# Roots by power on GpSimd, products on zeros, 64-row row sums and sums over consecutive words in an attention and expert kernel

## The reference

```
# a: retention, per sequence, 8 heads
h = layernorm(x)
q, k, v, g = h @ wq, h @ wk / 4, h @ wv, h @ wg;  q, k rotated
qk = (q k^T) * decay mask;  qk = qk / max(|rowsum(qk)|, 1)
out = qk v;  out = out * rsqrt(mean(out^2 per head) + 1e-5)
x = x + (silu(g) * out) @ wo
# b: hidden = layernorm(x); attention ACROSS the 8 sequences at each token position, causal, 16 heads, 4 kv heads
h1 = hidden + proj(attention(layernorm(hidden)))
# c, m: top 2 of 8 experts, with a capacity of 640 tokens an expert
ln2 = layernorm(h1);  gates = softmax over the top 2 of ln2 @ router
x = x + h1 + sum_e gate_e * gelu(ln2 @ w1_e) @ w2_e
```

## Time and profile before

| | |
|---|---|
| median of 3 runs | 242.56 us (239.90 to 242.67) |
| the profiled execution | 242.57 us, its span 240.8 us |
| busy: PE, PE weight loads | 216.7 us (90%), 183.6 us |
| busy: DVE, ACT, POOL | 180.1 us (75%), 146.1 us (61%), 94.8 us (39%) |
| ACT table loads | 36, of 1283 ns |
| chain that ended last | PE 54%, DVE 16%, issue 14%, POOL 9%, ACT 4% |

### The profile page before, as it was taken

How to read it: one execution, slowest core, us unless ns; L and a number is a source line. 1 busy time by engine, 2 the same in 40 slices (tenths; PEclk the granted TensorE clock), 3 DMA queues, 4 the chain that set the end, 5 groups by cost and what they waited for, 6 DMA issues and landing times.

```text
span 240.8 us, 4945 instructions
## 1 busy us (share of the span) xinstructions
PE 216.7 (90%) x1744; PEld 183.6 (76%) x1744; DVE 180.1 (75%) x543; ACT 146.1 (61%) x268; POOL 94.8 (39%) x121
## 2 busy tenths in 40 slices
PE   0677868899999999989999999999999989989995
PEld 0456545688887878877888889998798869879994
DVE  1466788695989789899996998697749864895533
ACT  2162763778868756946973876586746465827431
POOL 0021345334558642528623850582465136521000
PEclk9977999999999999999999999999999999999999
DMA  6992000000000000000000000000000000000000
GB/s 178 292 319 57 4 0 0 4 0 3 0 3 3 0 25 0 3 1 3 1 0 25 0 0 4 22 3 0 22 3 1 23 0 4 22 3 0 23 3 22
DMA packets 8073, 6.46 MB, mean 27 GB/s; under 512 B 752, under 2 KB 7152, under 8 KB 8048
## 3 DMA queue, kind: packets, MB, share of 16 engines
q1 hardware_dynamic: 8048, 6.14, 8.8%
HBM read 5.09 MB, written 1.05 MB: 25 GB/s over the span
## 4 chain that ended last, share of the span: by engine, by line
PE 54%; DVE 16%; issue 14%; POOL 9%; ACT 4%; DMA 1%; DVEq 0%; POOLq 0%; ACTq 0%
PE bank L773 16%; PE bank L784 13%; POOL prod L293 5%; PE bank L672 3%; DVE ao L930 3%; PE bank L621 3%; PE bank L699 3%; PE bank L638 2%; DVE res L1036 2%; PE bank L684 2%; ACT L445 2%; POOL qk L369 2%; PE bank L629 1%; PE bank L691 1%; DVE sm L866 1%
## 5 line engine op out<-in xcount | busy, mean ns | idle before, releaser
L773 PE MATMUL bank<-x2T,w 128*128 128x256 f32 x256 | 64.4, 386 | 1.6 <-DVE res L1036 1.6
L784 PE MATMUL bank<-w,hT 128*128 128x128 f32 x512 | 64.7, 277 | 0.0
L784 PEld LDWEIGHTS bank<-w,hT 128*128 128x128 f32 x512 | 61.7, 192 | 3.0 <-issue 1.1
L583 ACT ACTIVATE hT<-bank 128x512 f32<-128x512 f32 x64 | 37.5, 598 | 23.6 <-PE bank L773 23.5
L773 PEld LDWEIGHTS bank<-x2T,w 128*128 128x128 f32 x256 | 45.3, 190 | 8.1 <-DVE res L1036 3.1
L1036 DVE SCALAR_TENSOR_TENSOR res<-bank,gate,res 128x128 f32<-128x128 f32 x128 | 38.4, 341 | 16.7 <-PE bank L784 15.4
L445 ACT ACT_TABLE_LOAD x36 | 46.2, 1283 | 4.4 <-DVE mv L812 3.7
L293 POOL TENSOR_TENSOR prod<-qkv 128x128 f32<-128x128 f32 (+7 forms) x16 | 22.3, 1413 | 36.6 <-ACT qkv L455 36.6
L866 DVE TENSOR_TENSOR sm<-bank,con 128x512 f32<-128x512 f32 x32 | 19.9, 683 | 5.1 <-PE bank L672 5.0
L301 POOL TENSOR_TENSOR prodv<-attn_exp,qkv 128x128 f32<-128x128 f32 (+7 forms) x16 | 18.7, 1188 | 9.2 <-ACT attn_exp L551 9.2
L376 POOL TENSOR_TENSOR qkc<-qk,kcum 128x256 f32<-128x256 f32 x8 | 5.8, 730 | 31.0 <-DVE kcum L852 31.0
(11 more groups left out here) (109 smaller groups left out, 378.8 us busy)
## 6 DMA issues: line engine op xcount, KB each, us to landing
x<-in_x SPq DMA_DIRECT2D x8, 128.0 KB, 4.3
w<-in_w SPq DMA_DIRECT2D x1, 1024.0 KB, 5.8
out<-res SPq DMA_DIRECT2D x8, 128.0 KB, 1.8
con<-in_consts SPq DMA_DIRECT2D x1, 512.0 KB, 4.2
con<-in_consts SPq DMA_DIRECT2D x1, 256.5 KB, 4.3
con<-in_consts SPq DMA_DIRECT2D x1, 256.0 KB, 4.4
rcon<-in_rconsts SPq DMA_DIRECT2D x1, 132.0 KB, 2.9
wqk<-in_wqk SPq DMA_DIRECT2D x1, 128.0 KB, 2.2
```

Source lines behind the costliest of these rows:

```text
L583: eng.activation(hT[:, n % NM], m_banks[n % NM][:].rearrange("p (t n) -> p t n", t=NF), ACT.Gelu_apprx_tanh).then_inc(sem("gelu"), 1)
L773: last = mm(m_banks[n % NM][:, t * SLEN:(t + 1) * SLEN], w1[:, e, t * P:(t + 1) * P], x2T[:, i], start=True, stop=True)
L784: last = mm(m_banks[n % NM][:, c * D:(c + 1) * D], hT[:, n % NM, t, c * P:(c + 1) * P], w2[:, e, t], start=(t == 0), stop=(t == NF - 1))
```

## The change

- `a_rstd`, `b_rstd`, `c_rstd` leave ACT. GpSimd adds eps (`tensor_scalar`) and raises to -0.5 (`tensor_tensor` with `pow` against a broadcast constant). Three constants fewer for ACT's bias, one more for the exponent.
- A new stage `p_warm` on PE, eight times in the order: a product of zeros into the first expert bank. DVE clears `warm` at the start.
- `a_rowsums` multiplies only the 64 feature rows that belong to each half of the heads, into two banks (`front` joins f0 and f1), and so waits for `silu`; `a_scores` no longer does.
- For sequences 0 and 1 DVE does `a_qkc`, `a_weight`, `b_core` (straight from x1 with mean and root), `b_prod`, `b_prodv`.
- Scores, exponentials and V products are laid out with the sequence index `t` innermost, so `b_max`, `b_sum`, `b_ao` read consecutive words; `b_scores` writes with a stride, and `value_product` reads V with a stride of one sequence (192 words).
- The whole `ORDER` is written anew.

```diff
@@ ORDER (both listings are some 78 lines; the start of each)
-a_stats:0 a_aggr:0 a_rstd:0 a_xh:0 a_T:0 a_xT:0 a_qk:0 a_vmm:0 a_rotate:0 a_v:0 a_rotated:0 a_stats:1 a_kT:0
-a_aggr:1 a_knat:0 a_kcum:0 a_rstd:1 a_state_mm:0 a_stats:2 a_qkc:0 a_g:0 a_stats:3 a_state:0 a_aggr:2 a_xh:2
-a_rowsums:0 a_tanh:0 a_qo:0 a_silu:0 a_s2:0 a_xh:1 a_aggr:3 a_scores:0 a_mask:0 a_rstd:2 a_T:1 a_xT:1 a_qk:1
+p_warm:0 p_warm:1 p_warm:2 a_stats:0 p_warm:3 a_aggr:0 a_rstd:0 a_xh:0 a_T:0 a_xT:0 a_qk:0 a_vmm:0 a_rotate:0
+a_v:0 a_g:0 a_rotated:0 p_warm:4 a_tanh:0 a_kcum:0 a_kT:0 a_knat:0 a_qo:0 a_silu:0 a_state_mm:0 p_warm:5 a_qkc:0
+a_state:0 a_stats:1 a_rowsums:0 a_aggr:1 a_rstd:1 a_s2:0 a_scores:0 a_xh:1 a_stats:2 a_mask:0 p_warm:6 a_T:1
...
@@ GpSimd
+            def root(o, i_, n):
+                return eng.tensor_tensor(o, i_, minus_half[:].to_broadcast([P, n]), ALU.pow)
+
+            def b_rstd(i):
+                eng.wait_ge(sem("b_aggr"), NC * (i + 1))
+                eng.tensor_scalar(bln[:, i, :, 0], bmv[:, i, :, 1], EPS, None, ALU.add).then_inc(sem("b_var"), 1)
+                eng.tensor_scalar(bln[:, i, :, 1], bmv[:, i, :, 1], 1.0 + EPS, EPS * EPS,
+                                  ALU.mult, ALU.add).then_inc(sem("b_var"), 1)
+                eng.wait_ge(sem("b_var"), 2 * (i + 1))
+                root(br[:, i].rearrange("p c k -> p (c k)"), bln[:, i].rearrange("p c k -> p (c k)"),
+                     2 * NC).then_inc(sem("b_rstd"), 1)
...
@@ value_product
-                prodv[:, c, 0:n * D].rearrange("p (a d) -> p a d", d=HD),
-                attn_exp[:, c * n * NH:(c + 1) * n * NH].unsqueeze(2).to_broadcast([P, n * NH, HD]),
-                qkv[:, c, 0:n, D + KVD:QKV].unsqueeze(2).to_broadcast([P, n, QPK, KVD]), ALU.mult)
+                prodv[:, c, 0:n * D].rearrange("p (h d t) -> p h d t", d=HD, t=n),
+                attn_exp[:, c * n * NH:(c + 1) * n * NH].rearrange("p (h t) -> p h t", t=n)
+                .unsqueeze(2).to_broadcast([P, NH, HD, n]),
+                qkv[:, c, 0:n, D + KVD:QKV].rearrange("p t f -> p f t")
+                .unsqueeze(1).to_broadcast([P, QPK, KVD, n]), ALU.mult)
...
@@ TensorE
+            def p_warm(i):
+                if i == 0:
+                    eng.wait_ge(sem("warm"), 1)
+                mm(m_banks[0][:, 0:SLEN], warm[:, 0:P], warm[:], start=True, stop=True)
...
             def a_rowsums(i):
                 eng.wait_ge(sem("qkc"), i + 1)
                 eng.wait_ge(sem("state"), i + 1)
+                eng.wait_ge(sem("silu"), i + 1)
                 for u in range(2):
-                    last = mm(f1[:, u * SLEN:(u + 1) * SLEN], same_head[:, u * P:(u + 1) * P], qkc[:],
+                    rows = slice(u * D // 2, (u + 1) * D // 2)
+                    last = mm(front[:, u, 0:SLEN], same_head[rows, u * P:(u + 1) * P], qkc[rows, :],
                               start=True, stop=True)
...
@@ VectorE
+            def b_core(i):
+                if i < VECTOR_FIRST:
+                    eng.wait_ge(sem("b_rstd"), i + 1)
+                    if i >= 1:
+                        eng.wait_ge(sem("b_T"), i)
+                    for c in range(NC):
+                        last = ts_(core[:, c], x1[:, i, c], bmv[:, i, c, 0:1], br[:, i, c, 1:2], ALU.subtract, ALU.mult)
+                    last.then_inc(sem("core"), 1)
...
@@ b_scores, b_ao
-                    eng.tensor_reduce(sc[:, c * n * NH:(c + 1) * n * NH],
-                                      prod[:, c, 0:n * D].rearrange("p (a d) -> p a d", d=HD),
+                    eng.tensor_reduce(sc[:, c * n * NH:(c + 1) * n * NH].rearrange("p (h t) -> p t h", t=n),
+                                      prod[:, c, 0:n * D].rearrange("p (t h d) -> p t h d", t=n, d=HD),
                                       X, ALU.add).then_inc(sem("sc"), 1)
...
-                    eng.tensor_reduce(ao[:, c], prodv[:, c, 0:n * D].rearrange("p (t f) -> p f t", t=n),
+                    eng.tensor_reduce(ao[:, c], prodv[:, c, 0:n * D].rearrange("p (f t) -> p f t", t=n),
                                       X, ALU.add).then_inc(sem("ao"), 1)
```

More of the change, by code:

```diff
@@ L49 @@
[L49 to L53, removed]
@@ L276, in build @@
         res = sb("res", [P, NSEQ, NC, D])
-        ps = [ctx.enter_context(nc.psum_tensor(f"bank{i}", [P, 512], F32)) for i in range(8)]
+        front = ctx.enter_context(nc.psum_tensor("bankf", [P, 2, 512], F32))
+        ps = [front[:, 0], front[:, 1]] + [ctx.enter_context(nc.psum_tensor(f"bank{i}", [P, 512], F32))
+                                           for i in range(2, 8)]
         f0, f1, k0, k1 = score_banks = ps[:4]
@@ L455, in copy @@
                 eng.copy(o, i_).then_inc(sem(name), 1)
-            def a_rstd(i):
-                group = next(g for g in RSTD_GROUPS if g[0] == i)
-                eng.wait_ge(sem("a_aggr"), NC * (group[-1] + 1))
-                if i == 0:
-                    eng.wait_ge(sem("eps"), 2)
-                exp_ln()
-                js = slice(group[0], group[-1] + 1)
-                eng.activation(lnv[:, js], mv[:, js, :, 1], ACT.Ln, bias=eps[:, 0:1]).then_inc(sem("a_lnv"), 1)
-                eng.wait_ge(sem("a_lnv"), RSTD_GROUPS.index(group) + 1)
-                eng.activation(rstd[:, js], lnv[:, js], ACT.Exp, scale=-0.5).then_inc(sem("a_rstd"), len(group))
             def a_xT(i):
@@ L660, in a_scores @@
                 eng.wait_ge(sem("qo"), i + 1)
-                eng.wait_ge(sem("silu"), i + 1)
                 eng.wait_ge(sem("s2"), i + 1)
@@ L853, in a_kcum, with a_qkc, a_weight, b_prod @@
                                        ALU.add).then_inc(sem("kcum"), 1)
+            def a_qkc(i):
+                if i < VECTOR_FIRST:
+                    eng.wait_ge(sem("kcum"), i + 1)
+                    if i >= 1:
+                        eng.wait_ge(sem("rowsum"), i)
+                    tt_(qkc[:], qk[:, i % 2, 0], kcum[:], ALU.mult).then_inc(sem("qkc"), 1)
+            def a_weight(i):
+                if i < VECTOR_FIRST:
+                    eng.wait_ge(sem("rs"), i + 1)
+                    eng.wait_ge(sem("silu"), i + 1)
+                    tt_(wgt[:], rs[:], silu[:, i % 2], ALU.mult).then_inc(sem("wgt"), 1)
+            def b_core(i):
+                if i < VECTOR_FIRST:
+                    eng.wait_ge(sem("b_rstd"), i + 1)
+                    if i >= 1:
+                        eng.wait_ge(sem("b_T"), i)
+                    for c in range(NC):
+                        last = ts_(core[:, c], x1[:, i, c], bmv[:, i, c, 0:1], br[:, i, c, 1:2], ALU.subtract, ALU.mult)
+                    last.then_inc(sem("core"), 1)
+            def b_prod(i):
+                if i < VECTOR_FIRST:
+                    eng.wait_ge(sem("qkv_in_sb"), i + 1)
+                    if i >= 1:
+                        eng.wait_ge(sem("sc"), NC * i)
+                    for c in range(NC):
+                        key_product(eng, i, c).then_inc(sem("prod"), 1)
+            def b_prodv(i):
+                if i < VECTOR_FIRST:
+                    eng.wait_ge(sem("b_exp"), i + 1)
+                    if i >= 1:
+                        eng.wait_ge(sem("ao"), NC * i)
+                    for c in range(NC):
+                        value_product(eng, i, c).then_inc(sem("prodv"), 1)
             def a_state(i):
```

204 lines of the change are left out of this document (111 added, 93 removed).

## The result

The changed kernel takes 244.41 us (median of 4 runs, 243.48 to 246.57); the kernel before, run beside it, 241.23 (4 runs, 239.81 to 242.67). The ratio is 1.017, 95% interval 1.011 to 1.023. The forecast was 234.0 (228 to 240), so the time lies outside the range. Its profiled execution has a span of 244.8 us. The forecast as a ratio is 234.0/242.6 = 0.965, its range 0.940 to 0.989. The ratios leave disturbed runs out, the medians don't.

What follows compares the result with a forecast made beforehand. The prediction saw a chain of dependent small steps before 50 us and a nearly saturated matmul engine after (5.6 us idle). Gains of 5.0 us in front and 3.6 behind took 242.6 to 234.0 us, range 228 to 240.

Steps and rivals of the forecast that it cites:

- The first root: Front, first normalisation: addition and power on GpSimd take some 0.55 us instead of 1.86, giving back 1.3 us.
- the later ones: Later roots: two or three small ACT operations become as many small GpSimd ones, 0 on the path.
- The third rival: Roots on the path: the power is a long routine, ten times; at 2.5 us each the kernel takes 256.6; chance 0.12.
- Zeros first: Front: products on zeros keep the matmul engine's clock up, so early steps run at the higher level; 3.25 us gained.
- The first rival: Front: the clock does not rise early or falls again in the gaps; 237.2 us; chance 0.13.
- Gate product ahead of the row sums: Front, sequence 0: row sums now wait for the silu but no longer for the gate product; equal, 0.
- Row sums on 64 rows: Two halves side by side save 0.36 us a group: 0.45 in the front, 1.8 off the saturated engine after 50 us.
- First two sequences on DVE: Front: quicker weight product gains 0.6 us; DVE's extra work between 20 and 45 us loses 0.6.
- Consecutive words: Attention: shorter DVE sums and fewer ACT table loads give back a third of the engine's 5.6 us idle time, 1.8.
- the second rival: Attention: GpSimd pays for reading V with a stride, 6.0 us of its time; put at 239 us; chance 0.15.
- A third of the idle time: After 50 us: of the matmul engine's 5.6 us idle time, a third, 1.8 us, is given back.
- the front's 5.0 us: Before 50 us: 1.3 + 3.25 + 0.45 + 0.6 - 0.6 = 5.0 us gained.

Runs made afterwards that it cites:

- e2: The changed kernel with GpSimd's power replaced by a multiplication, so the roots are left out: 240.2 us, ratio 0.993 to the kernel before.
- e6: The changed kernel with GpSimd reading V in consecutive words, sums still consecutive, weights and V wrongly paired: 241.63 us, ratio 1.001.
- e7: The changed kernel with V read in words (wrongly paired) and a multiplication in place of the power: 236.31 us, ratio 0.984.
- w2: The changed kernel, whole, with V read in words, the products written with a stride, and eleven more products on zeros: 240.26 us, ratio 0.999.
- w4: The changed kernel with V read in words, products written with a stride, eleven more zeros, and a multiplication for the power: 237.67 us, ratio 0.987.
- h1: The kernel before with the eight products on zeros and nothing else: 241.23 us, ratio 1.003.
- after: The changed kernel itself, whole, set against the kernel before: 244.41 us, ratio 1.017.
- e5: The changed kernel with the row sums over all 128 rows again, still into two banks: 244.61 us, ratio 1.016.
- w1: The changed kernel, whole, with GpSimd's value product reading V in words and writing with a stride: 241.81 us, ratio 0.997.
- z1: The changed kernel, whole, with eleven more products on zeros in TensorE's idle time between 22 and 44 us: 244.47 us, ratio 1.015.
- v1: The changed kernel, complete, with ACT copying V into a tile of its own, sequence innermost: 243.38 us, ratio 1.011.
- w5: The changed kernel with V in words, strided product writes, eleven more zeros, and small additions before the later powers on VectorE: 240.22 us, ratio 1.000.
- e8: The changed kernel's code with the stages in the order of before, except those that would block for ever: 279.54 us, ratio 1.147.
- e3: The changed kernel with the old layout and a multiplication in place of the power: 242.72 us, ratio 1.000.

## Why the prediction was wrong, step by step

**The first root** (1.3 us) **and the later ones** (0): mis-sized, and with them the sign of the forecast. The normalisation starts at 4.77, 0.82 us earlier and not 1.3. "No row shows a power" was true, and taking the cheap end of 0.24 for each was the step that failed: a power of 2 elements with its handover takes 0.75 us (140.39 to 141.14 above), one of 4 elements 1.03 without it. "0 on the path" for the later roots went with it. The third rival had the mechanism, ten times on the path. By its rule, nine of 0.75 and one of some 1.06 lose 5.4 us (an estimate from these rows); e2 measured 5.8, but the same edit was worth 3.3 us in the old layout, 4.2 with V in words (e6 to e7) and 3.0 with the zeros as well (w2 to w4). I gave it 0.12 and discussed it as a long routine of 2.5 us. Its break-even of 1.1 us each held only if all 8.6 us were there to lose: half of them weren't.

**Zeros first** (3.25): right in mechanism. For the front as a whole, with cheap roots, 4.7 us of lead at gate 0 stand against 5.0 forecast, in a profile where the clock rose before the first query and key product, and 3.9 in e7, where it didn't (see the last section); the zeros' own size isn't seen apart, and h1 gives them 1.7 us in the kernel before. The power took 3.2 back (gate 0 at 50.0 instead of 46.9). The first rival, "falls again in the gaps", happened too (0.77 to 0.84 at 30 to 50 us): 1.4 us at the first gate by the profiles, less than the runs could tell. That the waits behind the front can also bring the clock down (0.69 at 160 to 165 us in after's profile) was in no rival.

**Gate product ahead of the row sums** (0): the row sums start at 12.35 instead of 15.12; nothing was lost by the new wait.

**Row sums on 64 rows** (0.45 and 1.8): the price is as forecast, the worth is not. Four instructions take 0.70 us in the timeline where e5's full rows take 1.03; the gain of 0.33 in five groups should be 1.6 us and doesn't show.

```profile
12.35 0.70 PE L679 MATMUL bankf<-qkc,con 64*128 64x256 f32 x4 [0.15 <-issue]
```

The step "off the saturated engine" failed as far as the profiles can tell. The likely reason is that the engine afterwards waits for the chain anyway (for gate and aon, 7.0 us after), so that shorter work becomes idle time; this is argued, as no run has full rows without those waits.

**First two sequences on DVE** (0.6 gained, 0.6 lost): neither is seen alone; the front's total fits.

**Consecutive words** (1.8): VectorE's half came as forecast (1215 ns), GpSimd's half came as the second rival had it. The rival's price for it, 0.7 ns an element, was 0.87 ns on the last sequence ((2866 - 1974)/1024). It was put at 6.0 us of GpSimd time and 239 us, 5 us above the forecast; it costs 4.7 us (after to w1), 3.8 (after to e6, and z1 to w2) or, with cheap roots, 2.1 (e2 to e7). The step that failed is that the sum had VectorE's gain from the layout and no price for GpSimd's read; the rival had it, at 0.15. The Trainium skill, "GPSIMD Engine Reference", section "Performance pitfalls for Q7 kernels", says that reads with a step above 8 bytes cost about half as much again; the trace agrees, with 45%. It does not cover v1, whose V is in neighbouring words and still takes 2352 ns.

**A third of the idle time** (1.8): failed even with the prices gone. In e7 and w4 the engine idles for 5.4 and 5.5 us behind the front, against 5.6. Taking ScalarE's 14 us of table loads away did not free anything: in the kernel before the engine waited for ScalarE only 0.2 us behind the front, and for VectorE's residuals and gate 1.6 and 1.4 (the waits above).

So the sum failed in three places. Of the front's 5.0 us, 3.9 to 4.7 are real with cheap roots. Of the 3.6 behind it, 0.7 is there at most: from the first gate to the end e7 takes 188.5 us and the kernel before 189.2. And two rivals that I had treated as alternatives, of 0.12 and 0.15, both came. Their prices came out differently from kernel to kernel: 3.0 to 5.8 us for the power, 2.1 to 4.7 for the read, 8.0 (0.033) for both from after to e7. Each such difference is uncertain by 2 us or more, so that a price depends on what else holds the chain is likely, not shown. From e7's gain of 3.9 us that leads back to after's loss of 4.1. That the range held e7 is luck in part: its two missing prices aside, the forecast was about twice too large.

## What to carry to other kernels

Before a function moves to another engine, ask for its price there for one element, not for the price of that engine's cheapest instruction: if no row has it, work out the break-even (here 1.1 us each, less if the gain is smaller than forecast) and see how near it lies to a plausible price. Mechanisms priced one by one as rivals can all happen, on one chain, so work out their sum too. When a layout is turned, look at who reads it and who writes it: let GpSimd write with a stride and read in words. Before work taken off a saturated engine is counted, see whether that engine waits soon after; here 1.6 us of it did not show. Before a forecast is made against one profile, see whether the kernel's other runs are like it: this one belonged to the slower of two groups, 2.7 us apart.

## What the runs showed of the hardware

- The power on GpSimd: 716, 1025 and 1652 ns for 2, 4 and 8 elements a partition.
- The same GpSimd product of 1024 elements takes 1960 to 1974 ns with V in words, 2153 with a strided write, 2352 with V and the products both in neighbouring words, the innermost axis over the sequences and the weights repeated over the one outside it, and 2866 with V read over 768 bytes.
- With the same four zeros ahead of the first transposes, the first query and key product took 1.13 us in 5 of the 16 profiles of the changed kernel and its variants (after, e2, e6, w2, w5; e8 in the old order is left out) and 2.07 or 2.08 in the other 11. w1's timeline:

```profile
5.48 0.69 PE L632 MATMUL bankf<-con,xh 128*128 128x128 f32 x2 [0.52 <-DVE xh L841]
6.63 2.07 PE L642 MATMUL bankf<-xT,wqk 128*128 128x256 f32 x4 [0.46 <-ACT xT L498]
```

  The first residual sum then comes at 28.1 us instead of 26.4 (w1 and w2). w5's twelve runs lie in two groups as well, at 240.0 to 240.3 and 241.7 to 242.1 us, about as far apart. e3's ten do too (240.8 to 240.9 and 242.7 to 242.9), at a granted clock of 1.00 throughout. Where a profiled execution had the slow first product it lies in the upper group (e3 242.9, w4 239.3 where the other six took 237.5 to 237.9), and w5's, with the quick one, in the lower. That the two go together is likely and wasn't shown: of the untraced runs no timeline exists.
- The kernel before has such groups as well, with different mean granted clocks: on three chips (those beside h1, w1 and w4) ten of the eleven runs counted at 1.00 took 239.7 to 239.9 us, and the five at 0.986 took 242.3 to 242.6.
- What holds the missing 5.5 us of the forecast in w4 is known in part: its idle time behind the front is that of the kernel before (of the 3.6 us behind the front 0.7 is there), and its eleven zeros cost 1.3 us at the first gate against e7. The rest stays open.
